# Three gather passes of a four-layer GNN kernel: every engine's program written out batch by batch, and the step to the next window moved to the passes' heads

## What is computed

```python
# layer 0: sum of source rows and edge features
agg = segment_sum(concat([h[src], edge_attr], 1), dst, N);  x += relu(concat([h, agg], 1) @ W0.T + b0)
# layer 1: edge softmax over destinations
pre = h[src] @ W_q + h[dst] @ W_k + edge_attr @ W_e + biases
alpha = segment_softmax(leaky_relu(pre) @ a_w + a_b, dst);  x += segment_sum(alpha * (h[dst] @ W_v + b_v), dst, N)
# layer 2: weighted sum of source rows
x += segment_sum(h[src] * (w * w2)[:, None], dst, N)
# layer 3: relation attention
x += relu(layernorm(segment_sum((h[src] @ W_r[type]) * mean_attn, dst, N) + bias) * g + b)
```

## Time and profile before

| | us |
|---|---|
| median of 3 runs | 8316.85 (8298.67 to 8347.98) |
| profiled execution, its own time | 8297.37 |
| its span, first to last instruction | 8295.3 |
| sum pass, first gather to last addition | 57 to 2322 |
| score pass | 2385 to 4940 |
| kept pass | 4974 to 5636 |
| attention pass | 5738 to 8230 |

### The profile page before, as it was taken

One profiled execution on the slowest core, in us unless ns is written; L12 is line 12 of the kernel. 1 busy time (PEld: TensorE's weight loads), 2 busy tenths in 40 slices (PEclk: granted clock), 3 DMA queues, 4 the chain that ended last, 5 costly groups with the idle time before them and its releaser, 6 DMA issues. The chain is left out here.

```text
span 8295.3 us, 160086 instructions
## 1 busy us (share of the span) xinstructions
PE 5185.0 (63%) x37998; PEld 3831.1 (46%) x38194; DVE 4646.3 (56%) x21263; ACT 4171.3 (50%) x11643; POOL 4948.9 (60%) x5713
## 2 busy tenths in 40 slices
PE   4666666666664444445445449996666666666664
PEld 3556555655552222222222228884444444444443
DVE  5555555555545454455445459996555555555556
ACT  3555555555524343344344349993555555555554
POOL 5555555555536556556556539993566666666663
PEclk7888888888876666666666669997666666666666
DMA  3333333333334444455444438884222222222221
GB/s 113 90 89 88 90 88 90 88 90 89 89 91 135 132 134 132 133 134 138 132 132 135 129 99 269 268 267 175 64 63 64 64 64 64 64 63 65 63 64 42
DMA packets 673100, 908.82 MB, mean 110 GB/s; under 512 B 141463, under 2 KB 430217, under 8 KB 672730
## 3 DMA queue, kind: packets, MB, share of 16 engines
q1 hardware_dynamic: 502654, 605.53, 23.3%
q0 software_dynamic: 168944, 301.30, 15.1%
q10 hardware_dynamic: 1357, 0.47, 0.0%
HBM read 696.57 MB, written 210.28 MB: 109 GB/s over the span
## 5 line engine op out<-in xcount | busy, mean ns | idle before, releaser
L801 POOL DMA_INDIRECT rows<-src_rows,idx_slots x1531 | 1469.1, 960 | 1007.9 <-issue 485.3
L801 POOL DMA_INDIRECT rows<-rel_rows,idx_slots x1531 | 1451.3, 948 | 967.3 <-remote 397.0
L801 POOL DMA_INDIRECT rows<-node_rows,idx_slots x1339 | 1279.3, 955 | 928.6 <-remote 338.6
L1399 ACT ACTIVATE onehot<-ident,fresh_slots 128x128 f32<-128x128 f32 x3136 | 993.0, 387 | 1501.5 <-remote 1079.1
L1390 PE MATMUL bank<-onehot,ones 128*128 128x512 f32 x1568 | 1317.0, 937 | 215.5 <-issue 129.8
L1097 ACT ACTIVATE dst_pairs<-pre,minus_node 128x512 bf16<-128x512 int16 x816 | 581.1, 718 | 1091.9 <-remote 589.5
L1488 PE MATMUL bank<-w_e,edge_in 128*128 128x256 f32 x784 | 405.8, 616 | 1045.7 <-remote 504.9
L1127 PE MATMUL bank<-by_chunk,dst_pairs 128*128 128x192 bf16 x6144 | 775.9, 270 | 301.8 <-issue 232.8
L1488 PEld LDWEIGHTS bank<-w_e,edge_in 128*128 128x128 f32 x784 | 210.5, 300 | 1438.3 <-issue 1103.9
L1127 PEld LDWEIGHTS bank<-by_chunk,dst_pairs 128*128 128x128 bf16 x6144 | 585.4, 108 | 381.0 <-issue 281.8
L1127 PE MATMUL bank<-wide_room,dst_pairs 128*128 128x192 bf16 x3264 | 477.6, 278 | 452.1 <-ACT dst_pairs L1101 255.6
(11 more groups left out here) (309 smaller groups left out, 11923.4 us busy)
## 6 DMA issues: line engine op xcount, KB each, us to landing
edge_in<-dst_line SPq DMA_DIRECT2D x392, 256.0 KB
spill<-rows SPq DMA_DIRECT2D x392, 256.0 KB
rows<-spill SPq DMA_DIRECT2D x392, 256.0 KB, 3.1
hot_rows<-rows SPq DMA_DIRECT2D x98, 712.0 KB
onehots<-hot_rows SPq DMA_DIRECT2D x196, 356.0 KB, 3.5
onehots<-src_low SPq DMA_DIRECT2D x98, 512.0 KB
edge_in<-in_ea_l SPq DMA_DIRECT2D x98, 256.0 KB
edge_in<-in_eaT_l SPq DMA_DIRECT2D x392, 64.0 KB
```

Source lines behind the costliest of these rows:

```text
L801: pool.indirect_dma_start(out=to[:, b.slot(ROW_RING), g, :], out_offset=None, in_=table, in_offset=bass.IndirectOffsetOnAxis(ap=idx[:, col ...
L1399: last = act.activation(diag[:, b.slot(2), g, :], ident[:, :], ACT.Copy, scale=fresh_slots[:, b.slot(2 * RING), g:g + 1])
```

## The change

In the sum, score and attention sweeps `pipeline` becomes `straight` for SP, ACT, PE and DVE: no register loop is left in them but the outer one over windows. The kept sweep keeps `pipeline`. The `_next` phases are gone. In their place DVE does the step at the head of each sweep (`next_window`), with the tables preset one window back; in score and attention PE waits for it before its first look-up, since PE reads `base` too. `reset_windows` no longer sets `dst_pairs`, and in the phase between score and kept pass ACT no longer does.

```diff
-                dve.tensor_copy(dst_rel[:, :], dst_rel0[:, :]).then_inc(s_set, 1)
+                dve.tensor_single_scalar(dst_rel[:, :], dst_rel0[:, :], float(WINDOW), ALU.add)\
+                   .then_inc(s_set, 1)
...
-        n_reset = 5
+        n_reset = 3
...
+        def next_window(dve, s_stepped, s_based, steps):
+
+            c = Chain(dve, s_stepped)
+            for step in steps:
+                step(dve, c)
+            dve.tensor_scalar(base[:, :], base[:, :], WINDOW, LAST_BASE, ALU.add,
+                              ALU.min).then_inc(s_based, 1)
+            dve.wait_ge(s_based, 1)
+
+        def windows_loop(sweep):
             windows = nc.values_load(n_windows[0:1, 0:1], min_val=1, max_val=N_PAD // WINDOW + 1)
             with nc.Fori(0, windows):
                 sweep()
-                with Phase(nc, name + "_next") as ph:
-                    s = ph.sem("set")
-                    block = ph.open()
-
-                    @block.vector
-                    def _(dve):
-                        c = Chain(dve, s)
-                        for step in steps:
-                            step(dve, c)
-                        c.do(dve.tensor_scalar(base[:, :], base[:, :], WINDOW, LAST_BASE,
-                                               ALU.add, ALU.min))
...
-                        pipeline(sp, [(0, stream), (0, line), (0, look),
+                        straight(sp, [(0, stream), (0, line), (0, look),
...
-                        pipeline(act, [(0, join), (6, hots)], unroll=GATHER_UNROLL)
+                        straight(act, [(0, join), (6, hots)], unroll=GATHER_UNROLL)
...
-                        pipeline(pe, [(0, sums), (0, lookups)], unroll=GATHER_UNROLL)
+                        straight(pe, [(0, sums), (0, lookups)], unroll=GATHER_UNROLL)
...
+                        next_window(dve, s_stepped, s_based, [next_places])
                         c = Chain(dve, s_parts)
...
-                        pipeline(dve, [(0, build), (6, hot0), (2, low), (6, hot1), (2, high),
+                        straight(dve, [(0, build), (6, hot0), (2, low), (6, hot1), (2, high),
...
                         fill_table(pe, w1_k, D, s_table, s_took)
-                        pipeline(pe, [(1, look), (6, spread)])
+                        pe.wait_ge(s_based, 1)
+                        straight(pe, [(1, look), (6, spread)])
...
+                        next_window(dve, s_stepped, s_based, [next_lane])
                         split_table(dve, Chain(dve, s_chain), D, 0, s_table, s_took)
-                        pipeline(dve, [(9, maxima), (4, join), (11, sums), (9, running), (4, leak),
+                        straight(dve, [(9, maxima), (4, join), (11, sums), (9, running), (4, leak),
...
+                        next_window(dve, s_stepped, s_based, [next_pairs, next_lane])
                         split_table(dve, Chain(dve, s_chain), D + N_ACTIVE, N_ACTIVE, s_table, s_took)
-                        pipeline(dve, [(3, maxima), (3, running),
+                        straight(dve, [(3, maxima), (3, running),
...
-                act.activation(dst_rel[:, :], dst_rel0[:, :], ACT.Copy).then_inc(s_places, 1)
-                for t in range(2):
-                    act.activation(dst_pairs[:, :, t], dst_rel0[:, :], ACT.Copy)\
-                       .then_inc(s_places, 1)
+                act.activation(dst_rel[:, :], dst_rel0[:, :], ACT.Copy, scale=1.0,
+                               bias=float(WINDOW)).then_inc(s_places, 1)
```

More of the change, by code:

```diff
@@ L660, in _ @@
                 dve.wait_ge(s_local, 1)
-                dve.tensor_copy(dst_rel[:, :], dst_rel0[:, :]).then_inc(s_set, 1)
-                dve.tensor_copy(base[:, :], base0[:, :]).then_inc(s_set, 1)
+                dve.tensor_single_scalar(dst_rel[:, :], dst_rel0[:, :], float(WINDOW), ALU.add)\
+                   .then_inc(s_set, 1)
+                dve.tensor_single_scalar(base[:, :], base0[:, :], -WINDOW, ALU.add)\
+                   .then_inc(s_set, 1)
                 dve.wait_ge(s_const, 14)
-                dve.tensor_copy(window_lane[:, :], lane[:, :]).then_inc(s_set, 1)
+                dve.tensor_single_scalar(window_lane[:, :], lane[:, :], float(-WINDOW), ALU.add)\
+                   .then_inc(s_set, 1)
                 dve.wait_ge(s_set, 3)
@@ L895, in far_stage @@
             return fars
-        n_reset = 5
+        n_reset = 3
         def reset_windows(pool, s_set):
[L901 to L906, removed]
+            for n, (to, of, by) in enumerate(((dst_rel[:, :], dst_rel0[:, :], float(WINDOW)),
+                                              (window_lane[:, :], lane[:, :], float(-WINDOW)),
+                                              (base[:, :], base0[:, :], -WINDOW))):
+                pool.tensor_single_scalar(to, of, by, ALU.add).then_inc(s_set, 1)
                 pool.wait_ge(s_set, n + 1)
@@ L956, in sweep @@
                     s_marks = ph.sem("marks")
+                    s_stepped, s_based = ph.sem("stepped"), ph.sem("based")
                     block = ph.open()
@@ L1457, in keep @@
                               .then_inc(s_spill[b.slot(ROW_RING)], 16)
-                        pipeline(sp, [(0, stream), (0, line_stage(sp, s_line, s_hot)),
+                        straight(sp, [(0, stream), (0, line_stage(sp, s_line, s_hot)),
                                       (3, index_stage(sp, a["src_l"], s_rows, s_idx)), (3, keep)],
@@ L1475, in exps @@
                                .then_inc(s_exp, 1)
-                        pipeline(act, [(5, spread_stage(act, s_score, s_diag, s_spread)),
+                        straight(act, [(5, spread_stage(act, s_score, s_diag, s_spread)),
                                        (6, far_stage(act, far1, RING, s_hot, s_far, s_max)),
@@ L1626, in _ @@
                     def _(sp):
-                        pipeline(sp, [(0, line_stage(sp, s_line, s_hot)),
+                        straight(sp, [(0, line_stage(sp, s_line, s_hot)),
                                       (3, index_stage(sp, rel_idx_rows, s_rows, s_idx))],
@@ L1655, in weigh @@
                             last.then_inc(s_weighted, 1)
-                        pipeline(act, [(2, far_stage(act, far3, 2, s_hot, s_far, s_spread)),
+                        straight(act, [(2, far_stage(act, far3, 2, s_hot, s_far, s_spread)),
                                        (3, shrinks),
@@ L1701, in _ @@
                         pe.wait_ge(s_ones, 1)
-                        pipeline(pe, [(1, look), (5, sum_up), (3, find), (2, spread)])
+                        pe.wait_ge(s_based, 1)
+                        straight(pe, [(1, look), (5, sum_up), (3, find), (2, spread)])
                     @block.vector
@@ L1947, in _ @@
             def _(pool):
-                pool.tensor_copy(window_lane[:, :], lane[:, :]).then_inc(s_set, 1)
+                pool.tensor_single_scalar(base[:, :], base0[:, :], -WINDOW, ALU.add)\
+                    .then_inc(s_set, 1)
                 pool.wait_ge(s_set, 1)
-                pool.tensor_copy(base[:, :], base0[:, :]).then_inc(s_set, 1)
-                pool.wait_ge(s_set, 2)
             @block.vector
```

10 lines of the change are left out of this document (5 added, 5 removed).

## The result

The changed kernel takes 8228.49 us (median of 4 runs, 8222.68 to 8236.28), the kernel before beside it 8309.76 us (4 runs, 8298.67 to 8347.98). The medians are 81 us apart. The ratio on record, which is not quite that of the two medians (0.9902), is 0.9891, with a 95% interval of 0.9871 to 0.9911, or 91 us (74 to 107). I had forecast 129 us. The profiled execution of the changed kernel took 8230.32 us with a span of 8228.5, against 8295.3 before: 67 us in this pair.

A forecast was written before the change was run, and what follows sets the result against it. No engine's throughput bound it; POOL waited between gather batches for others, slowed by costly sequencer instructions. Sum 37, score 79, attention 5 and phases 8 made 129 us off the 8316.85 median: 8188 us, range 8040 to 8330.

The forecast's parts named there:

- rival A: The forecast itself: one slow stretch in score is shortened and the rest holds, 8110 to 8270 us; chance 0.5.
- SP's 5.74 us: Mid-score: SP's time between an edge load and its next index load, cited for costly sequencer instructions in slow stretches.
- what I had listed as signs: Score gathers at 1.55 us or less, SP's DMAs 0.5 to 0.65 us apart, fewer DVE "issue" waits, packets over 600.
- Score: Score pass written out: 0.055 us less for each of 1434 gathers, 79 us (0 to 160).
- the head window: Score's written-out start: 96 gathers in 148.9 us, 1.551 us each, against the loop's 1.606.
- Sum: Sum pass written out: 0.029 us less for each of 1258 gathers, 37 us (0 to 60).
- Attention: Attention pass written out: 0.003 us less for each of 1434 gathers, 5 us (-35 to 50).
- Phases: `_next` phases between passes removed, DVE's step moved to the heads: net gain 8 us (bounds 0 to 12).
- The 4 us set aside: Attention's head: allowance for table matmuls delayed into the stretch where they come 2.5 us apart, up to some 10 us.
- Rival B: No difference: POOL's releases arrive late for reasons outside the programs; only the phases count, 8309 us; chance 0.2.
- rival C: Score's slow stretches feed themselves; half of POOL's 286.5 + 168.3 us of waits go, 8040 us; chance 0.2.
- Rival D: Slower: DVE's instruction fetches come late in slow stretches; at 1 us for each of 220 packets, 8408 us; chance 0.1.

The follow-up runs named there:

- with registers: Kernel before, score only: 32 steps written out, then a register loop of two rounds of 176 steps on SP, ACT, PE and DVE; ratio 1.0003.
- with edges: Kernel before with score written out in constants, plus short two-round register loops at every 8th step (16th on SP); ratio 0.9950.
- the repeat: The changed kernel itself, built and loaded again, against the kernel before; ratio 0.9893, 88 us less.
- plain score: Kernel before with only the score pass written out on its four engines; ratio 0.9958, 35 us less; two repeats 0.9955 and 0.9943.
- score with the additions of 0: Kernel before with POOL's tensor copies of base, lane and destinations between passes written as additions of 0; 8282.07 us in one run.

## Why the prediction was right, and where it was not

**The direction and the mechanism held.** The time fell by more than 0.5% and lies in the range, in rival A's band. The range, 290 us wide, would have held no change at all as well, so it is the ratio's interval that gives the direction. The reason given (a loop's step has more sequencer instructions, each costly in a stretch where POOL gathers) is what the runs with registers and with edges show for score, in the narrower form that values in registers cost and edges don't. My example for it was badly read: SP's 5.74 us hold four wait instructions of 0.70 us each and hardly any arithmetic. Nor has score's loop the 47 rounds of the prediction but 46. Most of what I had listed as signs came: 669 packets, SP's issues 0.60 to 0.72 us apart in mid-pass but for one, fewer "issue" waits on DVE, heads 0.5 and 1.2 us longer, and shorter ends. That no idle time stands beside the packets was not looked at packet by packet. One sign did not come. Gathers in score were to be at 1.55 us or less throughout; the profiled execution has 1380 in 2200 us, 1.594 each, hardly below the 1.602 of the kernel before, which I had listed as a sign of being wrong, and the repeat 1407, or 1.564.

**Score: the term was mis-sized by a factor of two.** 79 us came from 0.055 us per gather, the difference between the head window and the loop. The three measurements give 40 us. The step that failed is "I take the middle" of one window of 96 gathers: the five other traces shown first have 1.56 to 1.59 us there, and by those the loop's 1.606 leaves 0.02 to 0.05 us per gather. I had written that the head may show too little, as only SP was written out in all of it; it showed too much, by chance.

**Sum: mis-sized as well.** 37 us was forecast, the profiled pair shows 32, and it looked right. Measured by itself it is 8 us (21 less to 3 more), and the counts of 13 traces differ by 0.7% of the pass, 15 us. The agreement of one pair with one window was no confirmation.

**Attention: 5 us forecast, 14 measured by itself (2 to 27).** Within each group of measurements the counts over 2100 us differ by 3 to 7 gathers of 1350, 5 to 12 us of the pass. The forecast lies in it.

**Phases: 8 us forecast, 7 (18 less to 4 more) measured; in the pair of traces 12, or 13 from last gather to first, at my bound of 12 or just above.** Attention's end is 4.6 us shorter (4.8 forecast) and sum's 2.3 (2.6 forecast); attention's table begins 0.5 us later (3.74 against 3.27, 0.5 forecast), and sum's 1.2 (57.71 against 56.47 us), which I had priced at 1.5. The 4 us set aside for matmuls of the table that fall into a slow stretch were not needed. Over all traces the time from score's last gather to attention's first is 826 to 833 us with the step moved (four) and 836 to 843 without (ten).

**Rival B** (no difference, the releases are late for reasons outside the programs) is refuted by the time, yet its mechanism is real: POOL's 165.4 us of "remote" waits survived the writing out of score (168.3 before) and went only when gathers did. That is also why **rival C** could not come true: it took half of the join and "remote" waits from writing out alone, and they fell by 13 us in 168 and 30 in 286. **Rival D** (late fetches) did not show: the whole change is faster with 669 packets, and the kernel with edges has half as many q14 packets again as plain score and the same time. The Trainium skill ("Runtime: NRT & Kernel Launch", section "Instruction fetch mechanics") has it that crossing a block in order is mostly hidden; the 669 packets of the changed kernel agree.

In sum: 129 forecast; 40 + 8 + 14 + 7 = 69 by its parts, 88 to 91 as a whole. The 20 us between these two are within the errors, and no run settles them.

## What to carry to other kernels

Before pricing a one-per-cent gain from a stretch of one trace, find the same stretch in other traces: here one unchanged program's pass varied by 1.9%, more than the effect. Where a sequencer is pressed, write out what is computed in registers per step (wait values, DMA addresses); the loop itself may stay, if its values can be constants (shown for score alone). And where several engines show "issue" and "remote" waits together, look for a common cause, and test it by taking work away from that cause rather than from the engines that wait.

## What the runs showed of the hardware that I had not expected

- The median length of POOL's gathers is steady to the nanosecond within a pass (every hundred gathers have the same median; in all the traces one hundred, in score with the additions of 0, had 956 in place of 960) but depends on what POOL did before it: 946 and 944 ns in score and attention, 953 and 952 once POOL had done additions in place of copies between the passes. Another 1 to 4 ns, in all three passes about alike, came with the loading. Neither moved the kernel's time. Why an addition has this effect was not tried.
- Half the gathers cut a batch from 6.34 to 3.43 us, and DVE's and POOL's unexplained waits nearly vanished with them; TensorE's granted clock in that stretch was 0.89 in place of 0.66 (shares of 2.4 GHz, so both stretches mix its two levels, 1.2 and 2.4 GHz), and it was busy for 67% of the time in place of 50%. The window of the kernel with half the gathers (columns as in the earlier trace rows):

```profile
2500.00:3680.00 1180.00, 795.74 (x5554) 423.62 (x5552) 1035.84 (x6603) 889.59 (x2784) 697.33 (x696) 0.89 0.70 196
```

- 46 short register loops on each of three engines and 22 on SP, each with a jump back, cost nothing that could be measured in score (0.9950 with them, 0.9952 without).
